# Attention in a three-part block: transposes in groups of eight, both projections and both halves of values and outputs in one piece, inverse sums turned at the end of the slot

## The reference

```python
x = x + 0.5 * ffn(layernorm(x))      # slots of queries, 16 experts, combine
x = x + attention(layernorm(x))      # 16 heads of 64, rotary, causal
x = x + 0.5 * ffn(layernorm(x))
```

```python
q = rope(x @ Wq + bq);  k, v = split(x @ Wkv + bkv);  k = rope(k)
scores = where(causal, q @ k.T / 8, -inf)
out = softmax(scores) @ v
return out @ Wo + bo
```

## Time and profile before

| | us |
|---|---|
| median of 3 runs | 2754.2 (2752.78 to 2761.87) |
| profiled execution | 2756.2 |
| its span | 2754.4 |
| TensorE busy | 2563.0 (93%) |
| VectorE, ScalarE, GpSimd busy | 1761.7, 1621.5, 1443.1 |
| granted TensorE clock, mean | 0.976 |

### The profile page before, as it was taken

The page is one execution under the profiler, slowest core; times in us unless marked ns, Lnnn a source line. Parts: engine busy times, 40 slices in busy tenths (PEclk is TensorE's granted clock), DMA queues, the critical chain, the costliest instruction groups (busy, mean ns, idle before and its releaser), DMA issues. The chain is left out here.

```text
span 2754.4 us, 52948 instructions
## 1 busy us (share of the span) xinstructions
PE 2563.0 (93%) x17368; PEld 1929.3 (70%) x17368; DVE 1761.7 (64%) x3171; ACT 1621.5 (59%) x4049; POOL 1443.1 (52%) x1264
## 2 busy tenths in 40 slices
PE   7986999899999999999999999999999997987899
PEld 5752676677777777777777777777777774753576
DVE  5741577577676776666767766677677675751476
ACT  2321443577777777677777776777777772321343
POOL 1100443767667677676776766767667661100343
PEclk9998999999999999999999999999999998998999
DMA  7459553322223222232222222322223215359543
GB/s 240 151 222 401 191 157 117 69 42 60 48 54 63 47 51 50 50 62 47 55 62 47 55 47 51 64 45 52 50 52 63 46 39 199 122 196 413 188 153 104
DMA packets 164276, 290.98 MB, mean 106 GB/s; under 512 B 38176, under 2 KB 117664, under 8 KB 159904
## 3 DMA queue, kind: packets, MB, share of 16 engines
q1 hardware_dynamic: 164000, 287.57, 36.9%
HBM read 178.43 MB, written 41.94 MB: 80 GB/s over the span
## 5 line engine op out<-in xcount | busy, mean ns | idle before, releaser
L1501 ACT ACTIVATE att_prob<-att_ps_s,att_nmax 128x512 f32<-128x512 f32 (+3 forms) x1024 | 529.9, 528 | 282.9 <-DVE att_nmax L1408 282.9
L1309 POOL TENSOR_TENSOR att_z_sb<-att_z_sb,sh_vT 128x512 f32<-128x512 f32 x255 | 330.9, 1298 | 425.8 <-DMA att_zs<-att_z_sb 425.7
L1408 DVE TENSOR_REDUCE att_nmax<-att_ps_s 128x2 f32<-128x1024 f32 (+3 forms) x512 | 410.2, 822 | 13.3
L1650 PE MATMUL att_ps_p<-sh_ident,att_prob 128*128 128x128 f32 x2560 | 395.6, 277 | 22.9 <-DVE att_probT L1420 14.5
L1431 DVE TENSOR_TENSOR att_oT_lo<-sh_kT,att_oT_hi 128x512 fp32r<-128x512 f32 x128 | 130.9, 1022 | 410.1 <-ACT att_oT_hi L1531 410.1
L1312 POOL TENSOR_TENSOR att_z_sb<-att_z_sb,att_zs 128x512 f32<-128x512 f32 x255 | 339.4, 1331 | 20.0
L1650 PEld LDWEIGHTS att_ps_p<-sh_ident,att_prob 128*128 128x128 f32 x2560 | 290.3, 140 | 74.3 <-DVE att_probT L1420 28.9
L1310 POOL TENSOR_TENSOR att_zs<-att_zs,att_sin 128x512 f32<-128x512 f32 x255 | 330.9, 1298 | 0.0
L1661 PE MATMUL att_ps_p<-att_probT,att_v_sb 128*64 128x512 f32 (+3 forms) x2048 | 306.9, 442 | 3.7 <-ACT att_probT L1526 2.4
L1661 PEld LDWEIGHTS att_ps_p<-att_probT,att_v_sb 128*64 128x64 f32 x2048 | 138.3, 137 | 176.1 <-issue 136.2
L1526 ACT COPY att_probT<-att_ps_p 128x512 f32<-128x512 f32 x384 | 216.2, 601 | 57.6 <-PE att_ps_p L1650 56.5
(11 more groups left out here) (200 smaller groups left out, 5875.5 us busy)
## 6 DMA issues: line engine op xcount, KB each, us to landing
att_zs<-att_z_sb SPq DMA_DIRECT2D x1024, 64.0 KB, 2.3
ffn_w<-in_e_W SPq DMA_DIRECT2D x56, 1024.0 KB, 13.7
ffn_wg<-in_e_Wg SPq DMA_DIRECT2D x24, 1024.0 KB, 14.6
x_normalised_transposed<-dis_b_xnT SPq DMA_DIRECT2D x32, 512.0 KB, 3.0
dis_b_x<-in_x SPq DMA_DIRECT2D x16, 512.0 KB, 4.1
ex_w<-in_e_W SPq DMA_DIRECT2D x8, 1024.0 KB, 12.9
ex_wg<-in_e_Wg SPq DMA_DIRECT2D x8, 1024.0 KB, 16.4
sh_xt<-x_normalised_transposed SPq DMA_DIRECT2D x16, 512.0 KB, 4.6
```

Source lines behind the costliest of these rows:

```text
L1309: nc.gpsimd.tensor_tensor(z[:, m, i, :], z[:, m, i, :], cos[:], ALU.mult)
L1408: nc.vector.tensor_reduce(nmax[:, p % 2, qt, :], ps[:, :, at:at + (qt + 1) * P], AX.X, ALU.max, negate=True)\
L1501: nc.scalar.activation(prob[:, p % 2, hh, PLACE[qt]], ps[:, hh, at:at + (qt + 1) * P], ACT.Exp, bias=nmax[:, p % 2, qt, hh:hh + 1], accum_ ...
L1650: last = nc.tensor.transpose(turn_bank(p, k)[:, at:at + P], prob[:, p % 2, hh, PLACE[qt]][:, kb * P:(kb + 1) * P], g.ident[:])
```

## The change

The set of instructions stays; their order on three engines, the banks of the transposes and the counts waited for change. On TensorE Q and K are made in one piece; the transposes come as groups 1 and 2, then 3 and 4, then group 5 and the inverse sums at the slot's end; the scores' third unit stands between groups 2 and the values; both halves of a value product and of an output product are in one piece. On VectorE `copy_pt(1)` runs ahead of `low_part`. On ScalarE the copy of R is the slot's last work, the copies of values stand behind exps(1) and `copy_pt(4)`, and Q's high part directly behind K's. The constant `SPREAD = 6` gives the inverse sums the sixth place in the turn of banks.

```diff
-        turn_bank = lambda p, k: ps_p[(p + k) % 2]
+        turn_bank = lambda p, k: ps_p[(p + k + 1) % 2]
...
             def divide(j, p):
                 dve.wait_ge(pv_mm.sem, pv_mm.at(j, p + 1))
-                dve.wait_ge(pta_s.sem, pta_s.at(j, 4 * p + 1))
+                dve.wait_ge(pta_s.sem, pta_s.at(j, 4 * p + 4))
...
+                if t.has(p - 1):
+                    copy_pt(j, p - 1, 1)
                 if t.has(p - 2):
                     low_part(j, p - 2)
-                if t.has(p - 1):
-                    copy_pt(j, p - 1, 1)
...
                 if t.has(p - 2):
                     high_part(j, p - 2)
                 if t.has(p - 1):
-                    copy_r(j, p - 1)
+                    copy_pt(j, p - 1, 2)
                 if t.has(p + 1):
                     high(j, p + 1, 1)
-                if t.has(p - 1):
-                    copy_pt(j, p - 1, 2)
-                for u in t.values()[0:1]:
-                    values(j, u)
-                if t.has(p + 1):
                     high(j, p + 1, 0)
                 if t.has(p):
                     exps(j, p, 1)
-                    exps(j, p, 0)
-                for u in t.values()[1:]:
-                    values(j, u)
                 if t.has(p - 1):
                     copy_pt(j, p - 1, 4)
+                for u in t.values():
+                    values(j, u)
+                if t.has(p):
+                    exps(j, p, 0)
+                if t.has(p - 1):
                     copy_pt(j, p - 1, 5)
+                    copy_r(j, p - 1)
...
             def spread_sums(j, p):
                 pe.wait_ge(rec_s.sem, rec_s.at(j, p + 1))
+                pe.wait_ge(pta_s.sem, pta_s.at(j, 4 * p + 2))
...
             def transposes(j, p, k):
                 if k == 1:
+                    pe.wait_ge(exp_s.sem, exp_s.at(j, 8 * p + 8))
+                    need(pe, pta_s, j, 4 * p)
+                elif k == 2:
                     need(pe, on_s, j, p)
-                elif k in (2, 4):
-                    pe.wait_ge(pta_s.sem, pta_s.at(j, 4 * p + k // 2))
+                elif k == 4:
+                    pe.wait_ge(pta_s.sem, pta_s.at(j, 4 * p + 1))
...
                 if t.has(p + 2):
                     project(t, p + 2, 0)
-                if turned:
-                    spread_sums(j, p - 1)
-                if t.has(p + 2):
                     project(t, p + 2, 1)
                 if turned:
                     transposes(j, p - 1, 1)
-                for u in first_value:
-                    values(t, u, 0)
+                    transposes(j, p - 1, 2)
                 if t.has(p):
                     scores(j, p, 2)
-                if turned:
-                    transposes(j, p - 1, 2)
                 for u in first_value:
-                    values(t, u, 1)
+                    for half in range(2):
+                        values(t, u, half)
                 if turned:
                     transposes(j, p - 1, 3)
+                    transposes(j, p - 1, 4)
                 for u in t.values()[1:]:
                     for half in range(2):
                         values(t, u, half)
                 if out:
-                    output(t, p - OUT0, 0)
-                if turned:
-                    transposes(j, p - 1, 4)
-                if out:
-                    output(t, p - OUT0, 1)
+                    for half in range(2):
+                        output(t, p - OUT0, half)
                 if turned:
                     transposes(j, p - 1, 5)
+                    spread_sums(j, p - 1)
```

More of the change, by code:

```diff
@@ L1153, in attention_phase @@
     OFF = {}
+    SPREAD = 6
     TURNS = (None, ((0, 1), (0, 3)), ((0, 2), (1, 2)), ((1, 1), (1, 3)), ((0, 0),), ((1, 0),))
@@ L1417, in copy_pt @@
                 need(dve, pv_mm, j, p)
-                dve.wait_ge(pt_mm.sem, pt_mm.at(j, 6 * p + k + 1))
+                dve.wait_ge(pt_mm.sem, pt_mm.at(j, 6 * p + k))
                 a = OFF[TURNS[k][0]]
@@ L1506, in spread @@
                 act.wait_ge(inv_s.sem, inv_s.at(j, p + 1))
-                need(act, pt_mm, j, 6 * (p - 1) + 1)
+                need(act, pt_mm, j, 6 * p)
                 nc.scalar.copy(rinv[:], bcast(rsum[:], 3, ADH)).then_inc(rec_s.sem, 1)
@@ L1518, in copy_r @@
                 need(act, on_s, j, p - 1)
-                act.wait_ge(pt_mm.sem, pt_mm.at(j, 6 * p + 1))
-                nc.scalar.copy(R[:, p % 2, :], turn_bank(p, 0)[:]).then_inc(pta_s.sem, 1)
+                act.wait_ge(pt_mm.sem, pt_mm.at(j, 6 * p + SPREAD))
+                nc.scalar.copy(R[:, p % 2, :], turn_bank(p, SPREAD)[:]).then_inc(pta_s.sem, 1)
             def copy_pt(j, p, k):
                 need(act, pv_mm, j, p)
-                act.wait_ge(pt_mm.sem, pt_mm.at(j, 6 * p + k + 1))
+                act.wait_ge(pt_mm.sem, pt_mm.at(j, 6 * p + k))
                 a = OFF[TURNS[k][0]]
@@ L1635, in spread_sums @@
                 pe.wait_ge(rec_s.sem, rec_s.at(j, p + 1))
+                pe.wait_ge(pta_s.sem, pta_s.at(j, 4 * p + 2))
                 for qt in range(TT):
-                    last = nc.tensor.transpose(turn_bank(p, 0)[:, qt * P:(qt + 1) * P], rinv[:, qt].rearrange("p h e -> p (h e)"), g.ident[:])
+                    last = nc.tensor.transpose(turn_bank(p, SPREAD)[:, qt * P:(qt + 1) * P], rinv[:, qt].rearrange("p h e -> p (h e)"), g.ident[:])
                 last.then_inc(pt_mm.sem, 1)
@@ L1654, in mix @@
             def mix(j, p):
-                pe.wait_ge(pta_s.sem, pta_s.at(j, 4 * p + 4))
+                pe.wait_ge(pta_s.sem, pta_s.at(j, 4 * p + 3))
                 pe.wait_ge(ptv_s.sem, ptv_s.at(j, 2 * p + 2))
```

## The result

The changed kernel takes 2781.25 us (median of 4 runs, 2779.23 to 2782.35) against 2754.35 us: ratio 1.0091, interval 1.0072 to 1.0111. It is 27 us, 0.9%, slower. The profiled execution took 2779.23 us, its span 2777.2 us.

What follows compares the result with a forecast made beforehand. It took TensorE as the bound in attention. Terms of -0.5, -0.85, +1.7 and -0.1 gave +0.25 us an image, +3.8 over 15, plus 0.6 for the last image: +4.4, forecast 2759 us; range 2742 to 2782.

Steps and rivals of the forecast that it cites:

- likeliest case: Whole kernel: the forecast as summed, 2759 us, running from 2749 to 2769; chance 0.52, of it 0.42 within 0.3%.
- the clock falls in the new pause: Rival, turning slot: TensorE's clock falls in two of three pauses at 1.4 to 2.8 us, 2773 to 2787; chance 0.2.
- TensorE's own work: 0 a slot: All slots: same matmuls with other neighbours, so no cost taken; bounds 0 and +0.1 us a slot.
- Five plain slots, -0.5: Slots other than p = 4 to 6: 13.38 us becomes 13.28, -0.5 us an image; bounds -0.7 and +0.3.
- R late in plain slots: Rival, plain slots: R waits for `copy_pt(4)`, 0.3 us in each of 75 slots, +22, 2780; chance 0.12.
- tight chain: Plain slots: `low_part`, mask, reductions, exponentials, `copy_pt(4)` free R's bank at 12.65 us; TensorE comes to R at 12.7.
- The loading slot, 14.2 us: Slot p = 4: `copy_pt(1)` leaves the VectorE row up to `query_low`; 15.04 becomes 14.2 us, -0.85; bounds -1.4 and -0.6.
- The turning slot, +1.7: Slot p = 5: outputs wait for the late value copy, TensorE idle 1.8 to 1.9 us; +1.7 us an image, bounds +1.4, +2.0.
- I count no fall: Turning slot: TensorE's clock stays up behind the new pause of 1.8 to 1.9 us, so nothing is added.
- The slot after it, -0.1: Slot p = 6: transposes' waits go, R waits for exps(1) and `copy_pt(4)`; 12.65 us, -0.1; bounds -0.5 and +0.2.
- shorter normalisations: Rival, turning slot: normalisations under 3.5 us instead of 4.86, outputs wait 0.1 us, 2736; chance 0.14 including gains at their best.
- second rival: Turning slot: transposes don't count as clock activity, so longer runs next to a pause make a fall likelier; 2773 and more.

Runs made afterwards that it cites:

- e8: The kernel before with one swap on VectorE, `copy_pt(1)` ahead of `low_part`; TensorE's and ScalarE's orders of before: 2732.42 us, ratio 0.9907.
- e7: The changed kernel with the first value copy ahead of exps(1), the loading slot's statistics early and the normalisations split: 2718.10 us, ratio 0.9849.
- e9: The kernel before with `copy_pt(1)` ahead of `low_part`, statistics early and normalisations split; TensorE's and ScalarE's orders of before: 2702.47 us, ratio 0.9807.
- e5: The kernel of e1 with the loading slot's statistics and moments moved into VectorE's gap behind `divide`: 2738.02 us, ratio 0.9923.
- e10: The changed kernel with the turning slot's `low_part` behind largest(2) instead of ahead of it: 2746.45 us, ratio 0.9963.
- e3: The changed kernel with both value copies of ScalarE ahead of `copy_pt(4)`, still behind exps(1): 2786.80 us, ratio 1.0111.
- e4: The kernel before with ScalarE's copy of the first value product behind exps(1) and exps(0): 2826.22 us, ratio 1.0252.
- e1: The changed kernel with ScalarE's copy of the first value product ahead of exps(1) again: 2743.04 us, ratio 0.9954.
- e6: The changed kernel with the normalisations split, two behind `divide` and two behind `query_low`; value copies stay late: 2737.61 us, ratio 0.9925.
- e2: The changed kernel with VectorE's order of before, `low_part` ahead of `copy_pt(1)`: 2813.93 us, ratio 1.0210.

## Why the prediction was right or wrong, by its steps

Its likeliest case, no change to be told, did not come; its rival "the clock falls in the new pause", 2773 to 2787 with a chance of 0.2, did. The range held the time by less than a microsecond, and that was luck: its upper bound cut through this rival's own 2773 to 2787. One of the signs that the prediction named as showing it wrong, a clock that dips every image, came in 12 of 15.

- *TensorE's own work: 0 a slot.* Right. Slots without waits take 13.29 us in the new order and 13.27 in the old. Groups of eight, and projections in one piece, are worth nothing to TensorE itself.
- *Five plain slots, -0.5.* Right: -0.6; 13.28 to 13.31 at p = 0 to 3, as forecast. But the prediction gave the credit to K's earlier end together with the swap; e8 shows that the swap alone does it. Its rival "R late in plain slots" didn't come: no inverse sums waited at p = 0 to 3. The tight chain it named, R behind `copy_pt(4)`, does bind at p = 4 and 6, and is the one wait that e7 has and e9 hasn't; its 6.8 us are about half of what parts the two.
- *The loading slot, 14.2 us.* Right in its chain, 0.2 us too long: 13.99 measured, and e5 shows the chain. The rows that answer to the earlier trace rows, `copy_pt(1)`, `low_part` and `query_low` of the changed kernel:

```profile
1342.72 0.69 DVE L1422 COPY att_probT<-att_ps_p 128x512 f32<-128x512 f32 x1 [2.54 <-PE att_ps_p L1654]
1343.51 1.25 DVE L1433 TENSOR_TENSOR att_oT_lo<-sh_kT,att_oT_hi 128x512 fp32r<-128x512 f32 x1
...
1348.79 0.66 DVE L1388 TENSOR_TENSOR att_qT_lo<-att_z_sb,att_qT_hi 128x512 fp32r<-128x512 f32 x1
```
  `low_part` ends 9.30 into the slot (9.35 forecast).
- *The turning slot, +1.7.* Right in mechanism and place, wrong in size. First term: "`low_part` and `copy_pt(1)` only trade places". They do, but GpSimd's `key_low` starts 0.4 us sooner than before (9.18 us into the slot instead of 9.59), as K is projected and copied sooner, and `low_part` starts 0.6 later; it meets `key_low` and takes 1.17 us instead of 0.68. Before, these were the two instructions of this slot:

```profile
1352.64 0.68 DVE L1431 TENSOR_TENSOR att_oT_lo<-sh_kT,att_oT_hi 128x512 fp32r<-128x512 f32 x1
...
1352.80 1.67 POOL L1317 TENSOR_TENSOR att_kT_lo<-att_z_sb,att_kT_hi 128x512 fp32r<-128x512 f32 x1 [0.36 <-ACT att_kT_hi L1493]
```
  The prediction had K's earlier end and `low_part`'s wait for GpSimd in its plain slots, and didn't carry them to this one. Exps(1) start at 12.89 instead of 12.41, outputs at 15.02 instead of 14.43: 15 x 0.49 = 7 us come from `low_part`. e10 shows that this instruction is on the path.
- *The clock: "I count no fall".* This is the step that failed. It rested on one pause of 1.92 us that had no fall behind it, out of one. The changed kernel has 15 pauses of 2.33 to 2.35 us, 12 with a fall, at 1.6 us each: 19 us. Had the pause been 1.9 us as forecast, e3 and e4 say 8 or 9 falls, some 13 us, and 2772.
- *The slot after it, -0.1.* -0.2 measured; it depends on when ScalarE is done with the turning slot (e1: +0.6).
- *Rival: shorter normalisations.* Not what the change did, but e6, with two of the four moved away, shows the pause shrinking with them, to 1.1 us rather than the 0.1 of that rival.

With +4.4 as summed, 7 for `low_part` and 19 for the clock the sum is +30 on 2754: 2784, 3 above the measured median.

What stays open: which part of the new order costs the 0.5% that e1 and e7 show, why single plain slots grow by some tenths of a microsecond in e1, e5 and e7, and what decides whether the clock falls behind a given pause (no run changes the transposes next to a pause alone, which the prediction's second rival named).

## What to carry to other kernels

Where one engine works off a fixed list, place a copy that frees a bank by who waits for it in the slot with the latest neighbours, not in the plain slot: in seven of the changed kernel's eight slots nothing waited for the late value copy. Price a pause of TensorE at its length plus the clock: 1.25 us cost 1.3 (e10 against e1), 2.35 us cost 4.0 in four cases of five (the changed kernel against e1). Before regrouping the bound engine's work, try single swaps on the engines that feed it: one swap gave 0.9%, all VectorE moves together 1.9%, and the regrouping, with the order of ScalarE that goes with it, cost 0.5%.

## What the runs showed of the hardware that was not expected

The length of a pause doesn't settle alone whether TensorE's granted clock falls behind it. Of the pauses in turning slots, at 2.33 to 2.35 us it fell behind 12 of 15 (the changed kernel), at 1.84 to 1.90 us behind 8 of 15 and 9 of 14 (e3, e4), at 1.0 to 1.3 us behind none (15 each in e2 and e10, 12 in e6). But e2 has 14 pauses of 1.65 to 1.74 us and one of 2.46 with no fall, and in e4 one of the 1.19 us waits for `query_low`, of which the kernel before had 14 without a fall, was followed by one. The rows are, of e4, the wait and the stretch behind it, and, of e2, the longest pause and the stretch behind it (windows as above):

```profile
1606.88 0.50 PE L1628 MATMUL att_ps_s<-att_kT_hi,att_qT_hi 64*128 64x512 f32 x2 [1.19 <-DVE att_qT_lo L1386]
1607.50:1610.70 3.20, 3.20 (x14) 1.52 (x12) 2.47 (x5) 0.90 (x4) 3.12 (x4) 0.50 0.02 5
...
1844.28 0.55 PE L1654 MATMUL att_ps_p<-sh_ident,att_prob 128*128 128x128 f32 x3 [2.46 <-DVE att_probT L1422]
1844.40:1847.80 3.40, 2.40 (x20) 2.20 (x20) 3.37 (x5) 1.88 (x7) 1.79 (x2) 1.00 0.15 27
```
A slot with a fall was longer by 1.5 to 1.6 us in the mean than one without where the pauses were equal (19.49 against 17.99 in e3, 20.08 against 18.50 in the changed kernel).

VectorE's `low_part`, two inputs in SBUF, isn't stretched in proportion when it meets GpSimd; it ends about half a microsecond after GpSimd's running instruction: at 905.01 after `key_low` at 904.46, as at 1337.80 after 1337.26 in the earlier trace rows. Of 104 in the changed kernel that began while a GpSimd instruction ran, 94 ended 0.55 us after it. The same 512 columns take 0.69 us where GpSimd is idle. Where `low_part` began first, by 0.16 us at 1352.64 before, it took 0.68 us, and GpSimd's `key_low` took 1.67 instead of 1.29.
